# ScalarE reads the next group's number ahead of its wait for the products and copies the next gather's indices first

## The reference, cut to what matters

```python
# attention layer (twice: 2 heads of 128, then 1 head of 256)
e = el[src] + er[dst]
e = jnp.where(e > 0, e, NEG_SLOPE * e)
m = jax.ops.segment_max(e, dst, num_segments=num_nodes)
ex = jnp.exp(e - m[dst])
s = jax.ops.segment_sum(ex, dst, num_segments=num_nodes)
out = jax.ops.segment_sum(z[src] * (ex / s[dst])[:, :, None], dst, num_segments=num_nodes)
# mean aggregation (once)
msgs = x[src] * w[:, None]
agg = jax.ops.segment_sum(msgs, dst, num_segments=n)
wsum = jax.ops.segment_sum(w, dst, num_segments=n)
agg = agg / jnp.maximum(wsum, 1e-06)[:, None]
```

## Time and profile before

| | |
|---|---|
| median of 3 runs | 5531.81 us (5520.69 to 5536.3) |
| profiled execution, its own time | 5476.3 us |
| its span | 5474.4 us |
| mean granted TensorE clock over the span | 0.743 of full speed |
| busy, share of the span | PE 57%, VectorE 36%, ScalarE 27%, POOL 49% |
| walk 1 | 213 to 1540 us |
| walk 2 | 1640 to 2910 us |
| walk 3 | 3727 to 5035 us |

### The profile page before, as it was taken

One profiled execution on the slowest core, in us unless ns is written; L12 is line 12 of the kernel. 1 busy time (PEld: TensorE's weight loads), 2 busy tenths in 40 slices (PEclk: granted clock), 3 DMA queues, 4 the chain that ended last, 5 costly groups with the idle time before them and its releaser, 6 DMA issues. The chain is left out here.

```text
span 5474.4 us, 64894 instructions
## 1 busy us (share of the span) xinstructions
PE 3105.6 (57%) x13336; PEld 2063.1 (38%) x13336; DVE 1945.2 (36%) x5614; ACT 1503.9 (27%) x4807; POOL 2672.5 (49%) x2732
## 2 busy tenths in 40 slices
PE   4155555556652545455454489921555565656699
PEld 3144444444431222222223478810333333333466
DVE  4254455545432333233336822151222222222322
ACT  2122222222221222222221023311344344344223
POOL 1355556555516666666662145525656556551121
PEclk9567777777676777777775699965777777777799
DMA  6356566556623333333334256684444444442111
GB/s 152 82 91 106 96 101 102 97 105 102 98 54 96 93 94 93 94 91 95 92 94 124 73 192 221 220 233 127 113 114 117 113 114 116 114 112 71 54 56 57
DMA packets 381424, 598.27 MB, mean 109 GB/s; under 512 B 102442, under 2 KB 272078, under 8 KB 380658
## 3 DMA queue, kind: packets, MB, share of 16 engines
q0 software_dynamic: 136000, 386.29, 31.6%
q1 hardware_dynamic: 209138, 172.22, 11.7%
q10 hardware_dynamic: 36160, 38.56, 2.3%
HBM read 489.46 MB, written 107.34 MB: 109 GB/s over the span
## 5 line engine op out<-in xcount | busy, mean ns | idle before, releaser
L727 PE MATMUL walk_ps_part<-walk_rows,walk_whot 128*80 128x129 f32 (+1 forms) x4704 | 1109.6, 382 | 78.6 <-issue 78.5
L583 POOL DMA_INDIRECT walk_rows<-z_two_heads,walk_idx x784 | 779.2, 994 | 606.8 <-ACT walk_idx L597 375.1
L583 POOL DMA_INDIRECT walk_rows<-z_one_head,walk_idx x784 | 769.1, 981 | 569.2 <-ACT walk_idx L597 317.1
L1856 POOL DMA_INDIRECT walk_rows<-h,walk_idx x784 | 743.0, 948 | 523.9 <-ACT walk_idx L1870 270.1
L727 PEld LDWEIGHTS walk_ps_part<-walk_rows,walk_whot 128*80 128x80 f32 x4704 | 727.7, 186 | 343.1 <-issue 280.3
L2002 PE MATMUL walk_ps_part<-walk_rows,walk_whot 128*80 128x257 f32 x1568 | 498.2, 453 | 126.4 <-issue 84.2
L629 ACT ACTIVATE walk_window<-walk_ps_part 80x258 f32<-80x258 f32 (+1 forms) x196 | 74.8, 382 | 1225.8 <-remote 914.4
L620 ACT ACTIVATE walk_whot<-walk_hot,walk_w 128x80 f32<-128x80 f32 x1568 | 405.7, 346 | 20.8 <-ACT walk_w L611 15.0
L2002 PEld LDWEIGHTS walk_ps_part<-walk_rows,walk_whot 128*80 128x80 f32 x1568 | 250.3, 174 | 299.5 <-issue 249.5
L696 PE MATMUL walk_ps_row_scores<-keep_ident,walk_fmax 32*1 32x32 f32 (+1 forms) x98 | 18.4, 188 | 598.2 <-issue 312.9
L725 PE MATMUL walk_ps_part<-walk_window,walk_carry 80*1 80x129 f32 (+1 forms) x588 | 166.9, 372 | 158.4 <-issue 79.7
(11 more groups left out here) (365 smaller groups left out, 4661.4 us busy)
## 6 DMA issues: line engine op xcount, KB each, us to landing
exp_w<-in_ffn_W SPq DMA_DIRECT2D x108, 512.0 KB
agg<-walk_window ACTq DMA_DIRECT2D x198, 80.3 KB
walk_rows<-z_two_heads,walk_idx POOLq DMA_INDIRECT x784
walk_rows<-z_one_head,walk_idx POOLq DMA_INDIRECT x784
comb_ya<-y_tokens POOLq DMA_DIRECT2D x28, 448.0 KB
walk_rows<-h,walk_idx POOLq DMA_INDIRECT x784
walk_erB<-er_two_heads SPq DMA_DIRECT2D x104, 80.0 KB
agg<-walk_window ACTq DMA_DIRECT2D x99, 80.6 KB
```

The costliest lines, as they stand in the source:

```text
L583: pool.indirect_dma_start(out=Z[k // 2][:, k % 2 * GROUP_TILES + t, :], out_offset=None, in_=table, in_offset=bass.IndirectOffsetOnAxis(ap ...
L727: last = pe.matmul(P[k % 2][0:WIN, cols], S[k % HOTS][:, h, t, :], Z[k // 2][:, k % 2 * GROUP_TILES + t, h * HS:h * HS + HW], start=t == 0 ...
L1856: pool.indirect_dma_start(out=Z[k // 2][:, k % 2 * GROUP_TILES + t, :], out_offset=None, in_=table, in_offset=bass.IndirectOffsetOnAxis(ap ...
```

## The change

In both `edge_walk` and `mean_walk` the number of the group 8 steps on is read into a register at the head of `window`, beside n0 and ahead of the wait for `done8`. `copy_idx` no longer reads the number but takes it, and it runs directly behind the wait for `done8`: ahead of the wait for `stored`, of the copy of the sums and of the store. The number of instructions stays the same, and so does what each waits for otherwise.

```diff
@@ edge_walk
-            def copy_idx(s, k):
-                g = group(act, s)
+            def copy_idx(g, k):
                 act.activation(idx[k][:, :], keep["src"][:, bass.ds(g * GROUP_TILES, GROUP_TILES)],
                                ACT.Copy).then_inc(idx_ready, 1)
 
             def window(s, k, started):
-                n0 = first_node(act, s)
+                n0, after = first_node(act, s), group(act, s + UNROLL)
                 act.wait_ge(done8, s + (UNROLL + 1))
+                copy_idx(after, k)
                 if started is not None:
                     act.wait_ge(stored, started)
                 act.activation(wsb[k % 2][:, :], P[k % 2][0:WIN, 0:AW], ACT.Copy).then_inc(win_ready2, 1)
                 act.wait_ge(win_ready2, s + 3)
                 act.dma_start(agg[bass.ds(n0, WIN), 0:AW], wsb[k % 2][:, :]).then_inc(stored, 16)
-                copy_idx(s + UNROLL, k)
                 local(s + LOCAL_AHEAD, (k + LOCAL_AHEAD) % UNROLL)
@@
             for s in range(UNROLL):
-                copy_idx(s, s)
+                copy_idx(group(act, s), s)
@@ mean_walk
-            def copy_idx(s, k):
-                g0 = group(act, s)
-                act.activation(idx[k][:, :], keep["src"][:, bass.ds(g0 * GROUP_TILES, GROUP_TILES)],
+            def copy_idx(g, k):
+                act.activation(idx[k][:, :], keep["src"][:, bass.ds(g * GROUP_TILES, GROUP_TILES)],
                                ACT.Copy).then_inc(idx_ready, 1)
 
             def window(s, k, started):
-                n0 = first_node(act, s)
+                n0, after = first_node(act, s), group(act, s + UNROLL)
                 act.wait_ge(done8, s + (UNROLL + 1))
+                copy_idx(after, k)
                 act.wait_ge(stored, started)
                 act.activation(wsb[k % 2][:, :], P[k % 2][0:WIN, 0:HW], ACT.Copy).then_inc(win_ready2, 1)
                 act.wait_ge(win_ready2, s + 3)
                 act.dma_start(agg[bass.ds(n0, WIN), 0:HW], wsb[k % 2][:, :]).then_inc(stored, 16)
-                copy_idx(s + UNROLL, k)
                 local(s + LOCAL_AHEAD, (k + LOCAL_AHEAD) % UNROLL)
@@
             for s in range(UNROLL):
-                copy_idx(s, s)
+                copy_idx(group(act, s), s)
```

## The result

Beside the kernel before, the changed kernel takes 5363.85 us (median of 4 runs, 5358.6 to 5365.79) against 5526.65 us: ratio 0.9702, 95% interval 0.9684 to 0.972. That is 163 us by the medians. The profiled executions, 5358.6 and 5476.3 us, are 118 us apart, since the one of before lay 50 us under its median. What lies outside the walks took 5 us less in all. From its first index copy to its last window, walk 1 went from 1378.4 to 1367.8 us, walk 2 from 1271.5 to 1221.7, walk 3 from 1303.9 to 1251.8: 10.6, 49.8 and 52.1 us.

The account below looks back on a forecast made before the run. POOL's gather runs were taken to clock the walks in lock step. From 222 us (139 x 1.60), 77 us for caught second windows and 34 us for walk 3's slow read left 111 us: 5531.8 to 5421 us, range 5320 to 5590 us.

Parts of the forecast that it names:

- The lock step: All walks: POOL's gather runs set the clock; results seen 1.8 to 2.7 us after a run; 25.75 us a pair.
- 1.60 us off it: ScalarE: index copy takes the window copy's place, so release to first gather falls from 2.60 to about 1.00 us.
- The forecast of 111 us: Whole kernel: part of the gain, 222 - 77 - 34 = 111 us, giving 5421 us; chance 0.52.
- The upper bound, 222 us: All walks: 139 POOL idle times x 1.60 us; as the all-of-the-gain rival 5310 us, chance 0.15.
- the 1.6 that I had named as a sign: Sign of being right: POOL's idle time behind index copies down from 962 us by some 1.6 us each.
- Second windows caught: Walks 1 and 2: a pair's second window falls deeper into the run, giving runs of 8; costs 77 us of gain.
- more than 96 waits for the index copies: Sign of second windows caught: more runs of 8 gathers, POOL waiting for L597 more often than 96 times.
- 30 to 50 us: Sign of being right: walks 1 and 2 shorter by 30 to 50 us each.
- Walk 3, 34 us off for a slow read: Walk 3: the earlier group-number read may be slow on ScalarE; 0.8 us off 1.60, 43 times, 34 us.
- Slower: Rival: slow issue reaches ScalarE's eight activations in walk 3, or second windows are caught; around 5645 us, chance 0.20.
- No coupling: Rival: POOL's idle time is slack and earlier gathers give nothing; 5531.8 us, chance 0.13.

Follow-up runs that it names:

- e6: Kernel before, with TensorE's last matmul of every even group held until POOL has issued all gathers it was released for: 5517.77 us, ratio 0.9993.
- e5: Kernel after, unchanged, run on a chip where POOL never idles in a walk: 4662.14 us, ratio 0.9999 against the kernel before.
- e10: Kernel after's walk 3, with indices copied one group further ahead in walks 1 and 2, on a third chip: 5257.51 us, ratio 0.9613 against the kernel before.
- e8: Kernel before with indices copied one group further ahead, plus e6's hold: 5453.01 us, ratio 0.9881 against the kernel before without a hold.
- e7: Kernel after with e6's hold: 5349.85 us, ratio 0.9682 against the kernel before without a hold.
- e1: Kernel before with only the group number read ahead of the wait, index copy left behind window and store issue: 4659.07 us, ratio 0.9987.
- e2: Kernel after with the group number read behind the wait for the products, then index copy and window: 4662.24 us, ratio 0.9996.
- e12: Kernel before with POOL setting 128 x 288 numbers to zero ahead of each gather, to slow the gathers: 5135.84 us, ratio 0.9379.

## Why the prediction was right, and where it was not

*The lock step, and 1.60 us off it:* right. The step from release to gather is 1.01 us after (median of each walk), as forecast, and the period follows. e6 shows that results weren't used before the run was over, e5 that without the late release nothing is gained. Of the three walks with one period the prediction had shown two: a pair takes 27.3 us in walk 1.

*How near the sum came, and luck in it.* The forecast of 111 us lies 7 us from the profiled pair's 118 and 52 us under the medians' 163. The account below is of the traces: some 45 us of the 163 lie outside it, since the profiled execution of before was a quick one. Nor did the parts come out as forecast. Walks 1 and 2 gave 60 us in place of 77 (154 - 77), walk 3 gave 52 in place of 35 (69 - 34): two errors of 17 us that cancel. That the sum was near is partly luck.

*The upper bound, 222 us:* by the traces the times between release and gather add up to 367 us before and 144 after, 223 us less. Later releases took back 108 us of it: from the end of POOL's last gather of a run to the release, 438 us before and 545 after (61, 25 and 22 us more in the three walks). The runs took 9 us more. POOL's waits for the index copies fell from 6.9 to 5.9 us each (962.3 / 139, 882.2 / 149), 1.0 us and not the 1.6 that I had named as a sign, for the same reason. With the hold by hand the step was worth 168 / 222 = 0.76 of the bound.

*Second windows caught, 77 us off walks 1 and 2:* the size was near (96 x 1.60 = 154 us less the 60 measured = 94 us), the mechanism wrong. Runs of 8 in walk 1 became fewer (17 to 14), and in walk 2 they went from 2 to 4. The sign that I had named, more than 96 waits for the index copies, did come (103), and misled: it doesn't count runs of 8. The release comes late in walk 1, and where it does, another signal is seen late, L689's row scores for VectorE. There the step from release to gather fell by 84 us in sum; later releases (25 of 37 late ones in place of 7 of 31) took 61 us of it, and longer runs 13 us. That leaves 10 us, and 10.6 us were measured, where I had said 30 to 50 us. Walk 2 gave the 50 us at the upper end. I had looked only for the signal that ScalarE waits for; a signal of PE to VectorE within the run counts too.

*Walk 3, 34 us off for a slow read:* that term was wrong. The read lies in 9.47 us of idle time. But the release came 23.4 us after the run's start in place of 22.9 (medians), and 0.5 x 43 = 22 us off 69 leaves 47 us; 52 us were measured. Why it comes half a microsecond later I haven't found out. It needn't be the change: in e10, with the same walk 3 on another chip, it comes at 22.9.

*Slower:* no group of L1881 was over 3 us. The warning that signals caught by an earlier run can cost more than the start gains came true in e8's walk 3 (121 us slower than e7's).

*No coupling:* wrong for the chip of the comparison, right for the chip of e1 to e5. I gave it 0.13 as a doubt on the mechanism; that the same program has no late release on another chip I hadn't thought of. By the Trainium skill (SBUF — State Buffer, Who interferes with whom) no DMA contends with a compute engine. Nothing here contradicts it as to ports: the last packet of a gather in walk 3 of the kernel before ends 1.5 us behind the gather's issue at most places of a run. It is signals and issue that wait, and on these the rule says nothing.

*The separate worth of the earlier read and of the order* isn't settled: e1 and e2 ran only where POOL never idles.

## What to carry to other kernels

Before shortening a wait of the engine that sets the rhythm, list every signal that its run of work can overtake: an earlier start moves each of them deeper into the run, and a caught one with a chain behind it can cost more than the start gains (walk 3 of e8). If results are seen late while POOL issues indirect DMAs, test pacing them: here one gather each 1.47 us in place of 1.26 gave 6.2%, about twice what reordering ScalarE gave, though it should cost time on a chip without the delay (an estimate: the same 460 us, on 4662; not run there). And time a change on more than one chip before relying on it; this one is worth 3% or nothing.

## What the hardware showed that I had not expected

On three of four chips in the experiments, while POOL issues one indirect DMA of 128 rows each 1.26 us, the signals of PE are seen late by ScalarE and VectorE, and the release comes 1.4 to 1.5 us later for each gather since the run's start (an estimate from runs of 8, 16 and 24); on the fourth a signal takes 0.13 us in mid-run, and the same kernel takes 4663 us in place of 5471 to 5519. At one gather each 1.47 us the delay is gone there too.

The traces differ in one more thing. The kernel before's has 29,201 recorded updates of semaphores, and the other traces with the delay have 25,950 to 30,536. The five of the chip without it have 74,975 to 75,333, for the same number of DMA packets (some 381,400). Most of the missing ones lie in the walks (walk 1's gathers span 7116 records in the kernel before and 21,121 in e1). Paced e12 has 40,395: there the delay is gone, and over 30,000 records are missing still. So missing records and delay don't go strictly together. The timed runs have recorded spans too, so whether the recording has a part in the pile stays open. The Trainium skill (NOTIFIC — the notification-queue block, 7.1 Overflow: three behaviours, one of which stalls the engine) describes queues of such records that, when full, drop the new record, write over the oldest or hold up the producer. No run here shows that it is this.
